# Row numbers as integers in the gathered block, and five gathered blocks in place of two, in a cross-attention and expert kernel

## What is computed

```
logits = layernorm(x) @ gate_w.T;  probs = sigmoid(logits);  top 2 of 16 experts per token
weights = top_vals / (top_vals.sum(-1) + 1e-6)
slot    = expert * capacity + rank of the token in the expert   (capacity 320, further tokens are dropped)
h       = gelu(rows @ w1[expert]);  y = h @ w2[expert]          (256 -> 512 -> 256, per expert 320 rows)
x       = x + tanh(g_ffn) * sum over the 2 experts of weight * y
```

## Time and profile before

| | |
|---|---|
| median of 3 runs | 353.18 us (352.61 to 354.79) |
| profiled run | 354.84 us, its span 353.1 us |
| TensorE busy | 309.7 us, 88% of the span |
| VectorE, ScalarE, GpSimd busy | 240.8, 207.3, 209.1 us |
| DMA | 45.69 MB, mean 129 GB/s |
| granted clock of TensorE, mean | 0.953 |

### The profile page before, as it was taken

How to read it: one execution, slowest core, us unless ns; L and a number is a source line. 1 busy time by engine, 2 the same in 40 slices (tenths; PEclk the granted TensorE clock), 3 DMA queues, 4 the chain that set the end, 5 groups by cost and what they waited for, 6 DMA issues and landing times. The chain is left out here.

```text
span 353.1 us, 6283 instructions
## 1 busy us (share of the span) xinstructions
PE 309.7 (88%) x2081; PEld 268.8 (76%) x2083; DVE 240.8 (68%) x571; ACT 207.3 (59%) x569; POOL 209.1 (59%) x266
## 2 busy tenths in 40 slices
PE   8798999799999999997639799999999999999400
PEld 2456778699988889996624598999999999999400
DVE  1678887458877878776662199888778888886100
ACT  2465778578888887664460185666666666663200
POOL 7134238735578778775676106686666666766660
PEclk9999999899999999998969999999999999999855
DMA  6999998000012111111222848878778887753440
GB/s 183 267 310 257 179 181 199 16 18 16 17 45 72 66 47 45 48 48 46 75 91 75 244 146 238 210 192 198 190 200 201 218 201 200 190 98 42 51 52 8
DMA packets 40635, 45.69 MB, mean 129 GB/s; under 512 B 5445, under 2 KB 34650, under 8 KB 40602
## 3 DMA queue, kind: packets, MB, share of 16 engines
q1 hardware_dynamic: 33138, 35.78, 36.8%
q0 software_dynamic: 7424, 9.48, 15.1%
q10 hardware_dynamic: 40, 0.02, 0.0%
HBM read 28.02 MB, written 17.24 MB: 128 GB/s over the span
## 5 line engine op out<-in xcount | busy, mean ns | idle before, releaser
L530 POOL DMA_INDIRECT out_dram<-wqT,rows_to x48 | 78.9, 1643 | 51.9 <-issue 33.6
L1162 PE MATMUL ps_scores<-value_t,score_t 128*128 128x320 f32 x384 | 59.2, 310 | 0.5 <-DVE value_t L911 0.5
L1162 PEld LDWEIGHTS ps_scores<-value_t,score_t 128*128 128x128 f32 x384 | 56.4, 188 | 1.0 <-DVE value_t L911 1.0
L1075 PE MATMUL ps_scores<-score_t,xn 128*128 128x512 f32 x192 | 54.7, 430 | 0.0
L1109 PE MATMUL ps_out<-value_t,pT 128*128 128x256 f32 x384 | 53.2, 290 | 0.1
L1109 PEld LDWEIGHTS ps_out<-value_t,pT 128*128 128x128 f32 x384 | 48.0, 193 | 0.8 <-DVE x L811 0.6
L1075 PEld LDWEIGHTS ps_scores<-score_t,xn 128*128 128x128 f32 x192 | 37.1, 193 | 7.1
L659 ACT ACTIVATE ps_scores<-ps_scores 128x640 f32<-128x640 f32 x30 | 20.6, 688 | 33.6 <-PE ps_scores L1162 33.6
L476 POOL TENSOR_TENSOR probs<-probs,norm 128x1024 f32<-128x1024 f32 x16 | 30.5, 1904 | 16.1 <-DVE norm L852 16.1
L453 POOL DMA_INDIRECT padded<-z,slot_row x32 | 33.8, 1056 | 9.2 <-issue 6.5
L633 ACT ACTIVATE probs<-ps_scores,row_low 128x64 f32<-128x64 f32 x128 | 38.0, 327 | 0.4 <-DVE row_low L884 0.4
(11 more groups left out here) (176 smaller groups left out, 658.5 us busy)
## 6 DMA issues: line engine op xcount, KB each, us to landing
raw<-in_L_ffn_w_dram SPq DMA_DIRECT2D x16, 512.0 KB, 5.2
wo_sb<-in_L_ffn_w_dram SPq DMA_DIRECT2D x16, 512.0 KB, 4.3
padded<-xg SPq DMA_DIRECT2D x2, 2064.0 KB, 28.8
xg<-padded SPq DMA_DIRECT2D x16, 258.0 KB, 2.7
out_dram<-x SPq DMA_DIRECT2D x16, 128.0 KB, 1.8
padded<-xg SPq DMA_DIRECT2D x1, 1032.0 KB, 29.5
xg<-padded SPq DMA_DIRECT2D x16, 64.5 KB, 2.5
wq_sb<-in_L_xattn_Wq_dram SPq DMA_DIRECT2D x1, 1024.0 KB, 8.1
```

The source lines that it names most:

```text
L530: pool.indirect_dma_start(out, bass.IndirectOffsetOnAxis(ap=rows_to[0:SLOTS[k], e, k:k + 1], axis=0), y[0:SLOTS[k], j, k], None, compute_o ...
L1075: op = pe.matmul(dst, xn[:, j, a, c], mv, start=False, stop=last)
L1162: op = pe.matmul(ps_scores[:, f, 0:CAPACITY], w1_hl(p, a)[:, c, f * P:(f + 1) * P], x_hl(p, b)[:, c], start=c == 0 and (a, b) == PARTS[0], ...
```

## The change

The token's number is written as an integer into `z2` and `padded`, bit for bit in the place of the float. The scatter of y reads its row numbers straight from the gathered block, and the copies of y read their scale straight from it. So `rows_to`, `slot_w`, the small instructions and `marked` are gone, and whoever waited for `marked` waits for the gather itself. The gathered block now stays in use until the scatter has landed. For that there are five blocks (`GATHERS`), in the room of `k_diag` and `v_diag`, which become one tile `diag`. The gathers of experts 0 to 4 are issued at once, and that of expert e+5 in loop step e, behind the weight loads of the step, when the scatter of expert e has landed (`added`). The rows for unused slots (`empty`) get a tile of their own, and one memset of the preamble goes.

```
-        xg = sb("xg", [P, 2, SLOT_TILES, ROW])
+        xg = diag[:, 0:GATHERS * SLOT_TILES * ROW].rearrange("p (r k w) -> p r k w", r=GATHERS, k=SLOT_TILES)
+        empty = sb("empty", [P, SLOT_TILES, ROW])
...
                 if exists(e, EXPERTS):
-                    wait(sp, xg_turned, e - 1)
-                    wait(sp, marked, e - 1)
-                    at = e * TOKENS
-                    sp.dma_start(xg[:, e % 2, 0:2], padded[at:at + 2 * P, :].rearrange("(k p) r -> p k r", p=P)
-                                 ).then_inc(fetched[e % 2], 16)
...
-            fetch(0)
-            fetch(1)
+                    n = e - GATHERS
+                    if n >= 0:
+                        sp.wait_ge(added[n % 2], SLOT_TILES * 16 * (n // 2 + 1))
+                    at, r = e * TOKENS, e % GATHERS
+                    sp.dma_start(xg[:, r, 0:2], padded[at:at + 2 * P, :].rearrange("(k p) r -> p k r", p=P)
+                                 ).then_inc(fetched[r], 16)
...
+            for e in range(GATHERS):
+                fetch(e)
...
                     sp.dma_start(raw1[:, n % 2], w1_load[n]).then_inc(w1_loaded[n % 2], 16)
-                    fetch(n)
+                if e >= 0:
+                    fetch(e + GATHERS)
...
-            pool.memset(xg[:, 1, 2], 0.0).then_inc(consts, 1)
...
-                done.done(pool.tensor_tensor(z2[:, at:at + 2, :, TOKEN], token[:, 2 * r:2 * r + 2, None].to_broadcast([P, 2, 2]),
-                                             zeros[:, 0:4].rearrange("p (k q) -> p k q", k=2), ALU.add))
+                done.done(pool.tensor_tensor(z2[:, at:at + 2, :, TOKEN].bitcast(I32), token[:, 2 * r:2 * r + 2, None].to_broadcast([P, 2, 2]),
+                                             zeros[:, 0:4].bitcast(I32).rearrange("p (k q) -> p k q", k=2), ALU.add))
...
-            def mark(e):
-
-                if exists(e, EXPERTS):
-                    pool.wait_ge(fetched[e % 2], 48 * (e // 2 + 1))
-                    done.mark(pool.tensor_scalar(rows_to[:, e], xg[:, e % 2, :, TOKEN], 0.0, None, ALU.add))
-                    pool.tensor_scalar(slot_w[:, e], xg[:, e % 2, :, WEIGHT], 0.0, None, ALU.add).then_inc(marked, 1)
...
-                mark(e + 2)
-                done.sync()
+                pool.wait_ge(fetched[r], 48 * (e // GATHERS + 1))
...
-                    pool.indirect_dma_start(out, bass.IndirectOffsetOnAxis(ap=rows_to[0:SLOTS[k], e, k:k + 1], axis=0),
+                    pool.indirect_dma_start(out, bass.IndirectOffsetOnAxis(ap=xg[0:SLOTS[k], r, k, TOKEN:TOKEN + 1].bitcast(U32), axis=0),
...
-                    act.wait_ge(marked, e + 1)
+                    act.wait_ge(fetched[e % GATHERS], 48 * (e // GATHERS + 1))
...
-                                           scale=slot_w[0:SLOTS[k], e, k:k + 1]).then_inc(y_ready, 1)
+                                           scale=xg[0:SLOTS[k], e % GATHERS, k, WEIGHT:WEIGHT + 1]).then_inc(y_ready, 1)
```

More of the change, by code:

```diff
@@ L36 @@
 RING = 6
+GATHERS = 5
 DUMMY = SLOT_TILES * P
@@ L101, in build @@
         wqT = sb("wqT", [P, HC, DIM])
-        k_diag = sb("k_diag", [P, HC, BATCH, P])
-        v_diag = sb("v_diag", [P, HC, BATCH, P])
+        diag = sb("diag", [P, 2 * HC * BATCH * P])
+        k_diag, v_diag = (diag[:, k * HC * BATCH * P:(k + 1) * HC * BATCH * P].rearrange("p (c b m) -> p c b m", c=HC, b=BATCH)
+                          for k in range(2))
         score_t = sb("score_t", [P, 2 * DC * BATCH * HK], F32R)
@@ L115, in build @@
         iota_f = sb("iota_f", [P, EXPERTS])
-        token = sb("token", [P, TILES])
+        token = sb("token", [P, TILES], I32)
         zeros = sb("zeros", [P, DIM])
@@ L271, in build @@
         w1_high, w1_low, w2_high, w2_low = (sem(n) for n in ("w1_high", "w1_low", "w2_high", "w2_low"))
-        fetched = [sem(f"fetched{k}") for k in range(2)]
-        marked = sem("marked")
+        fetched = [sem(f"fetched{k}") for k in range(GATHERS)]
         added = [sem(f"added{k}") for k in range(2)]
@@ L300, in build @@
         PAIRS = TILES // 2
-        CONSTS = 8
+        CONSTS = 7
         block = held.enter_context(nc.Block())
@@ L416, in _ @@
                       allow_small_or_imprecise_dtypes=True).then_inc(consts, 1)
-            pool.memset(xg[:, 1, 2], 0.0).then_inc(consts, 1)
-            done.done(pool.memset(empty, 0.0))
-            pool.iota(empty[:, :, TOKEN], pattern=[[P, SLOT_TILES]], base=TOKENS, channel_multiplier=1,
+            done.done(pool.memset(empty[:, :, :], 0.0))
+            pool.iota(empty[:, :, TOKEN].bitcast(I32), pattern=[[P, SLOT_TILES]], base=TOKENS, channel_multiplier=1,
                       allow_small_or_imprecise_dtypes=True).then_inc(empty_ready, 1)
@@ L509, in _ @@
             pool.wait_ge(spare_stored, 16)
-            def mark(e):
-                if exists(e, EXPERTS):
-                    pool.wait_ge(fetched[e % 2], 48 * (e // 2 + 1))
-                    done.mark(pool.tensor_scalar(rows_to[:, e], xg[:, e % 2, :, TOKEN], 0.0, None, ALU.add))
-                    pool.tensor_scalar(slot_w[:, e], xg[:, e % 2, :, WEIGHT], 0.0, None, ALU.add).then_inc(marked, 1)
-            for e in range(2):
-                mark(e)
             for e in range(EXPERTS):
-                j, i = e % 2, e // 2
-                mark(e + 2)
-                done.sync()
+                j, i, r = e % 2, e // 2, e % GATHERS
+                pool.wait_ge(fetched[r], 48 * (e // GATHERS + 1))
                 wait(pool, added[(j + 1) % 2], SLOT_TILES * 16 * (i + j))
@@ L685, in expert @@
                             act.activation(y_low[:, :], ps_misc[SLOTS[k]:, 0:DIM], ACT.Copy,
-                                           scale=slot_w[SLOTS[k]:, e, k:k + 1]).then_inc(y_lowered, 1)
+                                           scale=xg[SLOTS[k]:, e % GATHERS, k, WEIGHT:WEIGHT + 1]).then_inc(y_lowered, 1)
                         else:
                             act.activation(y[0:SLOTS[k], j, k], y_bank(e, k), ACT.Copy,
-                                           scale=slot_w[0:SLOTS[k], e, k:k + 1]).then_inc(y_ready, 1)
+                                           scale=xg[0:SLOTS[k], e % GATHERS, k, WEIGHT:WEIGHT + 1]).then_inc(y_ready, 1)
             expert_steps(expert)
@@ L944, in expert @@
                     wait(dve, added[j], SLOT_TILES * 16 * i)
-                    dve.wait_ge(marked, e + 1)
+                    dve.wait_ge(fetched[e % GATHERS], 48 * (e // GATHERS + 1))
                     dve.wait_ge(y_lowered, e + 1)
-                    dve.scalar_tensor_tensor(y[0:n, j, 2], y_bank(e, 2), slot_w[0:n, e, 2:3], y_low[:, :], ALU.mult, ALU.add
+                    dve.scalar_tensor_tensor(y[0:n, j, 2], y_bank(e, 2), xg[0:n, e % GATHERS, 2, WEIGHT:WEIGHT + 1], y_low[:, :], ALU.mult, ALU.add
                                              ).then_inc(y_last, 1)
@@ L1141, in turn @@
                     wait(pe, x_low, t)
-                    pe.wait_ge(fetched[j], 48 * (i + 2))
+                    pe.wait_ge(fetched[t % GATHERS], 48 * (t // GATHERS + 1))
                     for k in range(SLOT_TILES):
```

9 lines of the change are left out of this document (3 added, 6 removed).

## The result

The changed kernel takes 365.75 us (median of 4 runs, 363.85 to 366.76) against 353.99 us (median of 4, 352.61 to 361.31) for the kernel before in the same session: ratio 1.034, 95% interval 1.027 to 1.041. It is slower by 3.4%, as forecast in sign and range (358 to 386), but 6 us less slow than the 372.0 us predicted. The profiled run took 365.7 us.

The account below looks back on a forecast made before the run. GpSimd's scatters were taken to end the chain, with TensorE dense before. Later start, S(2) at 233.7, ten experts at 10.15 us, three at 7.61 and 13.84 gave span 371.9, 18.8 more: median 372.0 us, range 358 to 386.

Parts of the forecast that it names:

- The new wait and what stands behind it: On SyncE, gather e+5 and the loads behind it wait for C(e), closing a loop through split, y and scatter: 10.15 us an expert.
- C(e): On GpSimd, the landing of expert e's last scatter; C(0) was put at 222.6 us.
- D: Time of an expert's scatters, C(e) = S(e) + D: 7.61 us with nothing beside it, put at 9.2 in the loop.
- S(e): On GpSimd, the start of expert e's first scatter; S(12) was put at 335.2 us and S(15) at 358.0.
- cheap bound: Cheapest loop, D = 7.61 and load 3.7 us: 8.65 us an expert, time 355.6; a milder loop near it had chance 0.09.
- Five gathers ahead: At the start on SyncE: w1 of expert 2 issued at 202.0, landing 5.1 us later, moving S(0) by 1.8 us to 215.0.
- TensorE's clock: Half speed for 3 us in every expert would lose 1.5 us, giving 9.7, still under 10.15, so the sum does not change.
- TensorE idle ahead of the second product: In the expert stage, TensorE was to be idle about 2 us an expert there, at an expert in 10 us.
- Small instructions at nothing: Removing 32 small GpSimd instructions was taken at nothing where another wait is later, and 0.1 us once at the end.
- reads from the block at nothing: Integers for floats and scales read from the gathered block: taken as 0, bounded by 0.1 us an expert either way.
- The first rival: No stall, and GpSimd quicker without its small instructions: 3.3 us less, median 349.9 us, 0.9% faster; chance 0.08.
- The tail: After S(12) no gather waits: three experts at 7.61 us, then 13.84 us from S(15) to the end of the span.

Follow-up runs that it names:

- one step earlier: Changed kernel with only gathers 0 and 1 ahead of the first loads and gather e+4 issued in step e, waiting for scatter e-1: 363.43 us, ratio 1.024.
- three steps earlier: Changed kernel with gather e+2 behind the loads of step e from step 3 on, waiting for scatter e-3: 392.14 us, ratio 1.104.
- loads ahead of the scatter: Kernel with gather e+3 in step e, plus a wait for scatter e-2 at the step's head and weight loads before the gather: 358.7 us, ratio 1.000.
- two steps earlier: Changed kernel with gather e+3 behind the loads of step e, waiting for scatter e-2: 351.08 to 364.38 us; timed again 354.77 us, ratio 0.991.
- the wait alone: Kernel before, with SyncE waiting for the scatter of expert e behind the gather of step e, ahead of the next weight loads: 356.78 us, ratio 0.999.

## Why the prediction was right, and where its size was off

**The new wait and what stands behind it: right.** S(e+2) was put at C(e) + 11.1. Measured from S(3) to S(12) it is 11.1 on average (10.5 to 11.9), in the predicted pieces. SyncE names the landing, and ScalarE waits at the w1 split 11 times, once for the late start and ten times in the loop. It closed one expert later than I had it: S(2) came 8.25 us behind S(1), at TensorE's pace, without a wait for a load. The experiments confirm the cause: without the early wait the stage is 136.8 us, with the start undone it is still 152.9.

**The term that was mis-sized: D, the time from S(e) to C(e).** The prediction put 9.2 us and counted 10.15 us an expert. Measured, C(e) - S(e) is 7.4 us on average (6.9 to 8.3), and an expert takes 9.36. Over the five rounds from S(2) to S(12), by way of C(2), S(4) and so on, it is 7.3 + 11.4 where 9.2 + 11.1 stood: 5 x (-1.9 + 0.3) = -8 us, which is the whole distance of 371.9 to 364.0. Three steps led to 9.2:

- D was read as the distance from one expert's first scatter to the next one's. But between the landing and the next first scatter GpSimd itself takes 0.74 us (0.72 behind the gather's start). The first rows of "one step earlier" show it (the gather goes at 247.45, the scatter at 248.17), and so does the kernel before, where one landing releases ScalarE at 330.92 and the scatter starts at 331.64. SyncE does not pay it.
- D was interpolated to loads at 1.3 us behind S. Since the scatters landed sooner, the next S came 2.0 us after C(e) (9.36 - 7.4) and not 1, and the w1 loads fell between -1.4 and +1.2, at 0.3 on average.
- The dear end of the interpolation, the 9.94 us of expert 0, holds a first scatter of 2.22 us in place of 1.61, drawn out while VectorE subtracted (213.81 to 215.03), which has nothing to do with the place of its load. In the loop of the changed kernel no scatter is drawn out.

The first two could have been had from the kernel before. Its expert 3, with the load at 0.39, took 8.58; less 0.74 that is 7.84. With it an expert takes (7.84 + 11.1) / 2 = 9.5 us, S(12) is 233.7 + 94.7 = 328.4, and the span 365.1. Expert 3 is the row to whose loads the loop comes nearest; I had gone halfway to the dearer expert 0. That the measured time still lies in the range owes something to its width: the loop ran at 9.36 us an expert, nearer to its cheap bound of 8.65 than to the dear one of 11.0.

**Five gathers ahead: right in mechanism, smaller at S(0), dearer at S(1).** The timelines of SyncE, ScalarE and TensorE in the kernel after answer to the earlier trace rows:

```profile
202.42 0.59 SPq L389 DMA_DIRECT2D raw<-in_L_ffn_w_dram  x1
```

```profile
206.71 1.06 ACT L659 ACTIVATE score_t<-raw 128x1024 fp32r<-128x1024 f32 x1 [1.74 <-DMA raw<-in_L_ffn_w_dram]
```

```profile
214.26 5.31 PE L1152 MATMUL ps_scores<-value_t,score_t 128*128 128x320 f32 x24 [1.81 <-DVE value_t L901]
```

The load was issued at 202.42 (202.0 predicted), but ScalarE had it 4.3 us later, not 5.1, and S(0) moved by 0.8 us instead of 1.8. Then TensorE waited 1.81 us and ran its next product at half speed, 5.31 us instead of 3.68. With its wait that took S(1) from 223.13 to 225.06 and S(2) along with it. So the 2.4 us at S(2), near the predicted 2.8, are the start and the clock, and not the loop's first round. That the two come out alike is luck.

**TensorE's clock: no change in the loop, right; ahead of it the clock cost S(1) some 1.6 us (5.31 - 3.68).** The window of that product (columns as in the earlier trace rows; 215 and 217 read the same):

```profile
216.00:217.00 1.00, 1.00 (x5) 1.00 (x5) 0.86 (x2) 0.00 (x0) 1.00 (x1) 0.50 0.91 96
```

It is the only such fall from S(0) to the last products. From S(2) to S(12) the granted clock is 1.00. The Trainium skill (TensorE: Matmul & The Clock Gate, section HAM oscillation — how this bites in real kernels) describes a kernel that starts every tile slow after a wait of some 3 to 5 us on a DMA. Here the waits inside the loop were at most 1.3 us, shorter than those, and none of them was followed by a fall; the 0.50 level behind each wait of 4.0 to 4.7 us in "three steps earlier" agrees with it.

**TensorE idle ahead of the second product: wrong place.** It waits there 1.1 us in two waits between 230 and 330 us. The rest is ahead of the first product, for VectorE's low part of the rows. Waits of TensorE in the kernel after, from 195 us on, and one of them in its timeline:

```profile
PE ps_scores L1152 <- DVE value_t L901: 7.4, 7, 1.8
```

```profile
266.65 3.78 PE L1152 MATMUL ps_scores<-value_t,score_t 128*128 128x320 f32 x24 [1.25 <-DVE value_t L901]
```

ScalarE's late w1 split delays the steps behind it, and these reach TensorE through VectorE's queue. I had looked only at the accumulator that y frees. It changed no term, because the loop does not pass through TensorE.

**Small instructions at nothing, reads from the block at nothing: right** (136.9 against 136.8 us, and 136.8 to 137.0 us in kernels that read from the block). The first rival rested on a small GpSimd instruction drawn out by VectorE, which is in the rows but not on the path; what the Trainium skill (SBUF — State Buffer, section Who interferes with whom) says of such pairs agrees with those rows, but taking the small instruction out gave no time back. That the scatter's own instruction is drawn out in the same way was not in the prediction. The tail went as said: S(12) to S(15) in 7.7 us an expert and 13.9 us to the end.

## What to carry to other kernels

On an engine that issues DMAs in program order, a wait is paid by everything queued behind it. Before a buffer's reuse is tied to a late event, list what stands behind that wait and whether its path leads back to the same event; if so it is a loop, and its period is the sum once round divided by the experts it spans. Put such a transfer where its wait has long been met, and the urgent ones ahead of it (here: 3.4% lost with the gather ahead of the loads, nothing measurable with the same wait and the gather out of the way).

When a duration is read as the distance between two starts, subtract what the second engine adds of its own; and time a kernel whose runs lie far apart many times, since four runs can show one pattern only.

## What the runs showed of the hardware

- An expert's three scatters land in about 6.9 us alone (7.61 from start to start, less 0.74), 7.4 on average with the two 512 KB loads issued between 1.4 us ahead and 1.2 us behind their start (the kernel after), in 7.3 to 8.8 with the w1 load 0.3 ahead ("loads ahead of the scatter", experts 1 to 10), and in 8.2 to 9.6 with it 1.5 to 1.9 behind ("one step earlier"). With loads an eighth as large, 0.8 to 1.5 behind it, they land in 6.8 to 7.5. In "loads ahead of the scatter" and "one step earlier" VectorE also drew out some of the instructions.
- A scatter instruction of GpSimd, 1.4 to 1.6 us long, takes 1.7 to 2.5 us when a subtraction of VectorE with both inputs in SBUF lies over it (250.04 in "one step earlier": 2.23 us).
- From a landing to the start of a scatter that waits for it GpSimd takes 0.7 us; SyncE's gather goes at once, at the same time as an instruction of ScalarE that waits for the same landing (275.95 and 275.96 in "one step earlier", the scatter at 276.68).
- A wait of 1.81 us on TensorE (212.45 to 214.26) was followed by 3 us at a granted clock of 0.50, after some 27 us at full clock. So were waits of 2.28 us ("two steps earlier", timed again, up to 315.24) and 2.58 us ("one step earlier", up to 319.58); waits of up to 1.57 us were not. But neither was one of 1.88 us in the kernel before (up to 196.89) nor one of 2.35 us in "the wait alone" (up to 202.04): the length of a wait alone does not tell.
